# A ring of five row buffers in a graph kernel: two of them loaded from ScalarE's DMA queue instead of SyncE's

## The chip, the cores and the metric

The kernel runs on one core of one Trainium2 chip. The metric is device time in microseconds (us) of one execution. A core has five engines with instruction streams of their own: TensorE (PE in the profile), VectorE (DVE), ScalarE (ACT), GpSimd (POOL) and SyncE (SP). SP and ACT can both start DMA transfers; each has a queue of its own, which the profile calls q1 (SP) and q10 (ACT). The profile marks such issues as SPq and ACTq. The core has 16 DMA engines.

## The reference, cut to what matters

Four graph layers run one after another over 3125 nodes of 128 features and 103,125 edges. Each is followed by a residual and a layer norm. The change lies in the first one, a graph convolution (GCN):

```
def _L0_gnn_ref(x, edge_row, edge_col, edge_val, weight, b):
    xw = x @ weight
    msgs = edge_val[:, None] * xw[edge_col]
    out = jax.ops.segment_sum(msgs, edge_row, num_segments=N_NODES)
    out = jax.nn.relu(out + b)
    return out
...
x = _layernorm(x + _L0_gnn_ref(x, src, dst, edge_weight, ...), axis=-1)
x = _layernorm(x + _L1_gnn_ref(x, edge_index, ...), axis=-1)     # attention over edges (GAT)
x = _layernorm(x + _L2_gnn_ref(x, ..., edge_index), axis=-1)     # transformer-like attention
x = _layernorm(x + _L3_gnn_ref(x, edge_index, ...), axis=-1)     # two mean aggregations (SAGE)
```

## The kernel before, in words

The kernel turns the edge list into dense matrices. A first stage sorts out edge tables; a second builds, with one-hot matmuls, a matrix in DRAM that holds for each pair of nodes the number of edges and the sum of their weights. The two values are interleaved by runs of 100 columns, so one source row of weights is 32 runs of 100 floats (400 bytes each). The node count is padded to 3200, which gives NT = 25 row tiles of 128 rows.

The GCN sweep is the function `gcn_sums` (line 888) of `gcn_gat_rows`. For each of the 25 row tiles it multiplies the features of the tile's 128 source nodes with the tile's weights (128 x 3200) and adds up in the eight banks of PSUM, all of which it fills. In the profile these are 16 matmul records a tile at line 896. Three engines feed it:

- SP (lines 850 to 853) loads the tile's weights from DRAM, 1600 KB a tile, into a ring of UN = 5 buffers. Four are parts of `src_rows`, the fifth is a part of `count_t`, which is why the profile shows the loads and matmuls under two names. The issue of `load_rows` is line 683.
- POOL (lines 865 to 869) copies the tile's features into the ring `left`, also of five.
- PE (lines 891 to 898) waits for both, and adds one to `gcn_used` when it is done with a tile. `gcn_used` begins at 5, so the load and the copy of tile t wait until tile t - 5 is used up.

The loop runs over five laps of five tiles; buffer u holds tile lap * 5 + u. After its 25 loads SP goes on to `load(0, 0)` and `load(0, 1)`, the first two tiles of edge counts for the next layer (`count_pair` in the profile), and then waits for work of that layer.

ACT starts 14 small loads of weights and vectors at the head of the stage (lines 1170 to 1180), spreads a small vector (line 1183), loads the table for the square root (line 1185), and then waits until all 25 tiles are used (line 1186). With that it copies half of the sums out of PSUM (`take_sums`, line 1146), DVE the other half. From there on the next matmuls (line 902), the norm and the GAT layer follow.

In this text tile t means row tile t of the sweep, and 5k the first tile of lap k. The whole code of the functions around the change:

Of the kernel before, what the change touches and what calls it, by code (L numbers as in the profile page):

```python
# [25 lines left out]
NT = -(-N // P)  # L26
# [7 lines left out]
UN = 5  # L34
# [628 lines left out]
def hold(eng, sem, value, held):  # L663

    eng.wait_ge(sem, value)
    eng.sem_inc(held, 1)
# [14 lines left out]
def load_rows(sp, tile, matrix, t):  # L681

    return sp.dma_start(tile.rearrange("p (t h l) -> p t h l", t=1, l=SL), matrix[:, bass.ds(t, 1)])
# [14 lines left out]
def gcn_gat_rows(nc, k, heads, cols, e, count):  # L698

    with ExitStack() as ctx:  # L700
# [3 lines left out]
        def sem(name):  # L704
            return ctx.enter_context(nc.semaphore(name))
# [31 lines left out]
        ring = [src_rows[:, u, :] for u in range(HEADS)] + [  # L737
            count_t[:].rearrange("p t c -> p (t c)")[:, 0:NP]]
# [14 lines left out]
        gcn_in = [sem(f"gr_gcn_in{u}") for u in range(UN)]  # L753
# [23 lines left out]
        def is_super(g, which):  # L777
            return isinstance(g, int) and g == which

        def width(g):  # L780

            return 1 if is_super(g, LAST) else TWO
# [18 lines left out]
        def each_super(eng, work):  # L801

            work(0)
            with eng.Fori(1, LAST - 1) as g:
                work(g)
            work(LAST - 1)
            work(LAST)
# [7 lines left out]
        def counts_done(g):  # L815

            return g * 5 + (2 * width(g) + 1)

        @block.sync
        def _(sp):  # L820
            def load(g, j):
                load_rows(sp, count[:, j, :], k.count_rs, g * TWO + j).then_inc(loaded[j], 16)

            def store_node(g, h):
                n = TWO * (C + 1)
                hold(sp, kept, g * HEADS + (h + 1), held_sp)
                sp.dma_start(k.node_d[:, h, bass.ds(g * (TWO * (C + 1)), n)], node[:, h % TWO, 0:n]
                             ).then_inc(node_stored[h % TWO], 16)

            def super_tile(g):  # L830
                if not is_super(g, 0):
                    store_node(g - 1, HEADS - 1)
                if is_super(g, LAST):
                    for i in range(TWO):
                        sp.wait_ge(node_stored[i], LAST * TWO * 16)
                    sp.dma_start(count[:, 1, 0:HEADS * FULL_NODES].rearrange("p (h c) -> p h c", h=HEADS), k.node_d
                                 ).then_inc(nodes_in, 16)
                hold(sp, turned_n, counts_done(g), held_sp)
                hold(sp, masked, g * TWO + width(g), held_sp)
                if not is_super(g, LAST):  # L840
                    for j in range(width(g + 1)):
                        load(g + 1, j)
                hold(sp, taken_n, counts_done(g), held_sp)
                w = width(g) * P
                sp.dma_start(counts_out[:, :, bass.ds(g * WIDE, w)], count_t[:, :, 0:w]).then_inc(stored, 16)
                if not is_super(g, LAST):
                    for h in range(HEADS - 1):
                        store_node(g, h)

            with sp.Fori(0, NT // UN) as lap:  # L850
                for u in range(UN):
                    sp.wait_ge(gcn_used, lap * UN + (u + 1))
                    load_rows(sp, ring[u], k.weight_rs, lap * UN + u).then_inc(gcn_in[u], 16)
            load(0, 0)
            load(0, 1)
            each_super(sp, super_tile)
            sp.wait_ge(stored, SUPERS * 16)
            sp.wait_ge(nodes_in, 16)
# [217 lines left out]
        def _(act):  # L1076
# [67 lines left out]
            def take_sums(piece):  # L1144
                cut = slice(2 * piece * CW, 2 * (piece + 1) * CW)
                act.activation(agg[:, cut].rearrange("p (b c) -> p b c", c=CW), ps[:, 2 * piece:2 * piece + 2, 0:CW],
                               ACT.Copy).then_inc(sums_by_act, 1)
# [31 lines left out]
            for n, v in enumerate((k.L2_gnn_Wq, k.L2_gnn_Wk, k.L2_gnn_Wv, k.L2_gnn_Wo)):  # L1179
# [3 lines left out]
            act.activation(wide_watt[:], watt[:, 0:HEADS].unsqueeze(2).to_broadcast([P, HEADS, P]), ACT.Copy, scale=0.8  # L1183
                           ).then_inc(spread, 1)
            act.activation(out_t[:, 0:1], eps[:], ACT.Sqrt)
            act.wait_ge(gcn_used, UN + NT)
            take_sums(0)
            take_sums(2)
# [1168 lines left out]
```

## Time and profile before

| | us |
|---|---|
| median of 3 runs | 2210.5 |
| lowest, highest | 2206.9, 2212.16 |
| the profiled execution | 2211.6 |
| its span | 2209.8 |

| engine | busy us | share of the span |
|---|---|---|
| PE | 1856.7 | 84% |
| DVE | 1736.5 | 79% |
| ACT | 1195.8 | 54% |
| POOL | 120.4 | 5% |

The profile is that of one execution. The span goes from its first to its last instruction. The shares are averages over stages of different kinds; no engine is the busiest in all of them. Of the DMA traffic, 337.05 MB went through SP's queue and 2.20 MB through ACT's. The mean granted clock of PE was 0.958 of full speed. Rows of a timeline have the start and the length in us, then engine, line and operation, the tiles written and read, and in brackets the idle time before with what ended it.

### The profile page before, as it was taken

How to read it: one execution, taken by the hardware profiler on the slowest of the kernel's cores; microseconds unless marked ns; L12 is line 12 of the kernel's file. 1: busy time of each engine (PE TensorE's matmuls, PEld its weight loads, DVE VectorE, ACT ScalarE, POOL GpSimd, SP SyncE). 2: the span in 40 equal slices, each digit the busy share in tenths (PEclk: the TensorE clock that was granted, in tenths of full speed). 3: DMA queues.
4: the chain of work that ended last, by engine and by line, in shares of the span. 5: the costliest groups of instructions: out<-in, count | busy, mean ns of one | idle time of the engine just before them, and what ended most of it. 6: DMA issues, size and time to landing. Idle time of an engine off the chain costs nothing. (4 is left out here: it accounts for less than half of the span.)

```text
span 2209.8 us, 45503 instructions
## 1 busy us (share of the span) xinstructions
PE 1856.7 (84%) x17150; PEld 1419.5 (64%) x17151; DVE 1736.5 (79%) x1784; ACT 1195.8 (54%) x2210; POOL 120.4 (5%) x225
## 2 busy tenths in 40 slices
PE   3677776799788888988888888995899999799997
PEld 2666665444566666766676666774688888655655
DVE  5999997000689999999999999977688888677276
ACT  1666665000476777767776677765666666500202
POOL 4000000000000000000000000000000000011010
PEclk9999999899999999999999999985999999899999
DMA  4799998999043144413443144324355555299194
GB/s 114 220 255 255 256 256 231 264 272 272 4 121 81 43 120 120 120 31 91 120 120 69 54 121 120 92 62 102 78 119 119 119 119 149 100 380 392 56 404 165
DMA packets 482577, 341.91 MB, mean 155 GB/s; under 512 B 322696, under 2 KB 474528, under 8 KB 475856
## 3 DMA queue, kind: packets, MB, share of 16 engines
q1 hardware_dynamic: 476864, 337.05, 55.0%
q10 hardware_dynamic: 4928, 2.20, 0.4%
q0 software_dynamic: 720, 1.77, 0.3%
q8 instruction: 43, 0.70, 0.1%
q14 instruction: 22, 0.18, 0.0%
HBM read 214.05 MB, written 126.94 MB: 154 GB/s over the span
## 5 line engine op out<-in xcount | busy, mean ns | idle before, releaser
L1087 ACT ACTIVATE exponentials<-gr_ps,att_cols 128x256 f32<-128x256 f32 (+1 forms) x1300 | 486.7, 492 | 177.5 <-PE gr_ps L942 175.6
L942 PE MATMUL gr_ps<-ident,gr_r 128*128 128x128 f32 (+1 forms) x2500 | 369.2, 286 | 42.4 <-DVE gr_r L1293 40.3
L975 PE MATMUL gr_ps<-exponentials,heads 128*33 128x128 f32 (+1 forms) x5000 | 368.9, 283 | 35.2 <-DVE exponentials L1299 35.2
L1299 DVE SCALAR_TENSOR_TENSOR exponentials<-exponentials,gr_count_t 128x3072 f32<-128x3072 f32 (+1 forms) x104 | 344.0, 3307 | 25.8 <-ACT exponentials L1087 24.7
L1261 DVE CUSTOM_DVE_ANT_0 gr_unread<-gr_src_rows,gr_closed 128x3125 bf16<-128x3125 f32 (+1 forms) x100 | 341.3, 3413 | 17.2 <-ACT gr_src_rows L1141 12.5
L942 PEld LDWEIGHTS gr_ps<-ident,gr_r 128*128 128x128 f32 (+1 forms) x2500 | 274.3, 145 | 124.2 <-issue 105.7
L975 PEld LDWEIGHTS gr_ps<-exponentials,heads 128*33 128x33 f32 x5000 | 258.8, 115 | 103.3 <-issue 50.5
L577 PE MATMUL bm_ps<-bm_hot 128*96 128x100 bf16 x4224 | 223.6, 210 | 99.0 <-DVE bm_hot L527 99.0
L577 PEld LDWEIGHTS bm_ps<-bm_hot 128*96 128x96 bf16 x4224 | 206.4, 124 | 116.5 <-DVE bm_hot L527 116.5
L611 ACT ACTIVATE bm_stage<-bm_ps 96x800 f32<-96x800 f32 x264 | 207.1, 830 | 115.9 <-PE bm_ps L577 108.7
L527 DVE TENSOR_TENSOR bm_hot<-bm_hot,near 128x2304 bf16<-128x2304 bf16 x132 | 179.2, 1358 | 18.9
L1293 DVE TENSOR_SCALAR gr_r<-gr_src_rows,gr_bounds_u 128x3125 f32<-128x3125 f32 (+1 forms) x100 | 187.9, 1920 | 7.4 <-DVE gr_bounds_u L1280 4.0
L2035 PE MATMUL sage_ps<-sage_counts,sage_parts 128*128 128x400 bf16 x960 | 164.0, 332 | 0.0
L1574 PEld LDWEIGHTS ar_ps<-ar_values,ar_pt 128*128 128x128 f32 x1250 | 147.1, 194 | 11.2 <-ACT ar_pt L1655 2.5
L1574 PE MATMUL ar_ps<-ar_values,ar_pt 128*128 128x128 f32 x1250 | 149.4, 277 | 0.0
L1555 PE MATMUL ar_ps<-XT,ar_left 128*128 128x400 f32 x400 | 142.8, 500 | 1.9 <-issue 1.7
L2035 PEld LDWEIGHTS sage_ps<-sage_counts,sage_parts 128*128 128x128 bf16 x960 | 93.9, 98 | 68.5
L523 DVE TENSOR_TENSOR bm_hot<-low_grid,near 128x1600 bf16<-128x1600 int16 x132 | 130.0, 985 | 1.6 <-PEq L562 0.9
L896 PE MATMUL gr_ps<-gr_src_rows,exponentials 128*128 128x400 f32 x320 | 114.9, 514 | 17.0 <-DMA gr_src_rows<-adjacency 16.6
L1220 DVE COPY gr_r<-gr_ps 128x800 f32<-128x800 f32 x2 | 1.9, 986 | 155.3 <-PE gr_ps L896 155.3
L1655 ACT ACTIVATE ar_pt<-ar_ps 128x512 f32<-128x512 f32 (+1 forms) x175 | 82.5, 548 | 76.1 <-PE ar_ps L1564 76.1
L896 PEld LDWEIGHTS gr_ps<-gr_src_rows,exponentials 128*128 128x128 f32 x320 | 60.6, 194 | 71.4 <-issue 30.1
(307 smaller groups left out, 1998.7 us busy)
## 6 DMA issues: line engine op xcount, KB each, us to landing
adjacency<-bm_stage SPq DMA_DIRECT2D x264, 300.0 KB, 3.4
count_pair<-adjacency SPq DMA_DIRECT2D x37, 1600.0 KB, 8.5
count_more<-count_by_source SPq DMA_DIRECT2D x30, 1600.0 KB, 8.5
count_by_source<-gr_count_t SPq DMA_DIRECT2D x12, 3200.0 KB, 17.3
gr_src_rows<-adjacency SPq DMA_DIRECT2D x20, 1600.0 KB, 15.0
count_pair<-count_by_source SPq DMA_DIRECT2D x20, 1600.0 KB, 8.5
count_more<-adjacency SPq DMA_DIRECT2D x13, 1600.0 KB, 8.4
gr_count_t<-adjacency SPq DMA_DIRECT2D x5, 1600.0 KB, 15.0
```

The lines of the kernel that those rows point to most:

```text
L527: dve.tensor_tensor(planes(2, PARTS)[:, :, 0:KEYS], key.to_broadcast([P, PARTS, LW // 2, 2 * KEYS]), near(2, PARTS)[:, :, 0:KEYS], ALU.mul ...
L577: last = pe.matmul(place(i, plane), key, hot[:, u, 1, a, :, b], start=i % PER_BANK == 0 and plane == 0, stop=True, skip_group_check=True)
L611: act.activation(stage[:, u, HALF_LW * h:HALF_LW * (h + 1)].rearrange("p (b w) v c -> p b (w v c)", b=HALF_BANKS), ps[0:KEYS, bank:bank + ...
L896: last = pe.matmul(ps[:, b, 0:CW], left[:, u, :], ring[u][:, b * CW:(b + 1) * CW], start=False, stop=True, skip_group_check=True)
L942: last = pe.transpose(ps[:, i % RINGS, c:c + n], r[0:n, slot(g, h) + j, s * P:(s + 1) * P], k.ident[0:n, 0:n])
L975: last = pe.matmul(ps[j * PAIR:j * PAIR + C + 1, 7, 0:rows(g)], heads[:, h, s, :], e[:, s, c:c + rows(g)], start=s == 0, stop=s == NT - 1, ...
L1087: last = act.activation(e[:, s, places(g, h)], ps[:, i % RINGS, c:c + w], ACT.Exp, bias=cols[:, h, s:s + 1])
L1261: dve.tensor_tensor_reduce(out=unread[:, 0:n], in0=src_rows[:, h, 0:n], in1=closed[:, j, 0:n], scale=1.0, scalar=FLOOR, op0=ALU.subtract, ...
L1293: last = dve.tensor_scalar(r[:, slot(g, h) + j, 0:n], src_rows[:, h, 0:n], bounds_u[:, 1, h, j:j + 1], bounds_u[:, 0, h, j:j + 1], ALU.add ...
L1299: dve.scalar_tensor_tensor(part, part, 1.0, count_t[:, first:last, places(g, 0)], ALU.min, ALU.mult).then_inc(weighed, 1)
L1574: last = pe.matmul(ps[:, 7, 0:D], pt[:, i, j * P:(j + 1) * P], values[:, first + j, :], start=first + j == 0, stop=first + j == NT - 1, sk ...
L2035: last = pe.matmul(ps[:, b, 0:CW], part, right[:, columns(b)], start=opens and i == 0, stop=True, skip_group_check=True)
```

## The change

SP's loop over the ring now takes only the buffers 0, 2 and 4. ACT gets a loop of its own for the buffers 1 and 3, with the same waits, the same transfers and the same semaphores. It stands behind ACT's last preparation and ahead of its wait for the end of the sweep.

```diff
@@ -848,7 +848,7 @@
             with sp.Fori(0, NT // UN) as lap:
-                for u in range(UN):
+                for u in range(0, UN, 2):
                     sp.wait_ge(gcn_used, lap * UN + (u + 1))
                     load_rows(sp, ring[u], k.weight_rs, lap * UN + u).then_inc(gcn_in[u], 16)
             load(0, 0)
@@ -1183,6 +1183,10 @@
             act.activation(out_t[:, 0:1], eps[:], ACT.Sqrt)
+            with act.Fori(0, NT // UN) as lap:
+                for u in range(1, UN, 2):
+                    act.wait_ge(gcn_used, lap * UN + (u + 1))
+                    load_rows(act, ring[u], k.weight_rs, lap * UN + u).then_inc(gcn_in[u], 16)
             act.wait_ge(gcn_used, UN + NT)
             take_sums(0)
             take_sums(2)
```

What stands on SP at the end of its loop over the ring (`gr_src_rows` are buffers 0 to 3, `gr_count_t` is buffer 4):

```order
 L852 REGISTER_ALU
 L683 ISA [waits gr_gcn_used]
-L683 DMA gr_src_rows<-adjacency 128x32x100
-L852 REGISTER_ALU
-L683 ISA [waits gr_gcn_used]
-L683 DMA gr_src_rows<-adjacency 128x32x100
-L852 REGISTER_ALU
-L683 ISA [waits gr_gcn_used]
 L683 DMA gr_count_t<-adjacency 128x32x100
 L850 REGISTER_ALU
```

Two of the five loads of a lap have left SP, each with its wait. The count tiles that follow the loop stay where they were.

What stands on ACT between the square root's table load and its first copy of the sums:

```order
 L1185 ACTIVATE gr_out_t<-gr_eps 128x1
+L1186 UNCONDITIONAL_BRANCH
+L1186 ISA
+L683 ISA [waits gr_gcn_used]
+L683 DMA gr_src_rows<-adjacency 128x32x100
+L1188 REGISTER_ALU
+L683 ISA [waits gr_gcn_used]
+L683 DMA gr_src_rows<-adjacency 128x32x100
+L1186 REGISTER_ALU
+L1186 COMPARE_AND_BRANCH
 L1146 ACTIVATE gr_r<-gr_ps 128x800 [waits gr_gcn_used]
```

The loop body with two loads and two waits now stands where ACT had only the wait for the end of the sweep.

## Rows read from the trace of the kernel before

**Rows 1.** The page: span, and GB/s in 40 equal slices.
```profile
span 2209.8 us, 45503 instructions
...
GB/s 114 220 255 255 256 256 231 264 272 272 4 121 81 43 120 120 120 31 91 120 120 69 54 121 120 92 62 102 78 119 119 119 119 149 100 380 392 56 404 165
```

**Rows 2.** Windows in the sweep: stretch, length, busy time of engines, clock, DMA, GB/s.
```profile
core 0: us, PE busy (x) PEld busy (x) DVE busy (x) ACT busy (x) POOL busy (x), PEclk, DMA share, GB/s
...
420.00:450.00 30.00, 28.14 (x82) 14.75 (x81) 0.00 (x0) 0.00 (x0) 1.48 (x5) 1.00 1.28 273
...
510.00:540.00 30.00, 28.08 (x81) 14.73 (x80) 0.00 (x0) 0.00 (x0) 0.59 (x2) 1.00 1.29 272
```

**Rows 3.** Timeline of POOL in the sweep: start us, length us, what.
```profile
405.84 0.30 POOL L869 COPY exponentials<-X 128x128 f32 x1 [18.23 <-PE gr_ps L896]
411.31 0.30 POOL L869 COPY exponentials<-X 128x128 f32 x1 [5.18 <-PE gr_ps L896]
416.59 0.30 POOL L869 COPY exponentials<-X 128x128 f32 x1 [4.98 <-PE gr_ps L896]
...
512.46 0.30 POOL L869 COPY exponentials<-X 128x128 f32 x1 [5.72 <-PE gr_ps L896]
518.48 0.30 POOL L869 COPY exponentials<-X 128x128 f32 x1 [5.73 <-PE gr_ps L896]
```

**Rows 4.** Line 896, the sweep's matmuls: counts, and what they waited for.
```profile
L896 PE MATMUL gr_ps<-gr_src_rows,exponentials x320: 499/499/1031, 397.4 to 541.9; 128*128 128x400 f32 x160
...
  DMA gr_src_rows<-adjacency: 16.6, 16
```

**Rows 5.** SP's issues in the sweep, then the row loads to landing.
```profile
383.83 22.74 SPq L683 DMA_DIRECT2D gr_src_rows<-adjacency  x4
...
527.72 5.60 SPq L683 DMA_DIRECT2D gr_count_t<-adjacency  x1
...
L683 SPq DMA_DIRECT2D gr_src_rows<-adjacency x20: 667/5692/10325, 383.8 to 521.6; - x20
...
DMA to landing us min/median/max: 13.4/15.0/19.5
```

**Rows 6.** Timeline of PE: the sweep's first tiles, and its last.
```profile
397.36 24.71 PE L896 MATMUL gr_ps<-gr_src_rows,exponentials 128*128 128x400 f32 x64 [10.98 <-DMA gr_src_rows<-adjacency]
...
542.75 5.64 PE L896 MATMUL gr_ps<-gr_count_t,exponentials 128*128 128x400 f32 x16 [0.37 <-DMA gr_count_t<-adjacency]
```

**Rows 7.** Timeline of ACT around the sweep.
```profile
383.52 0.39 ACTq L1170 DMA_DIRECT2D gr_gcn_w<-in_L_gnn_weight_dram  x1
...
393.32 0.91 ACTq L1180 DMA_DIRECT2D wjoin<-in_L_gnn_Wo_dram  x1
...
396.27 0.20 ACT L1185 ACTIVATE gr_out_t<-gr_eps 128x1 f32<-128x1 f32 x1
548.42 1.57 ACT L1146 ACTIVATE gr_r<-gr_ps 128x800 f32<-128x800 f32 x2 [151.94 <-PE gr_ps L896]
```

**Rows 8.** Both queues at work: windows, then packets and MB of each in 4:5.
```profile
4.00:5.00 1.00, 0.00 (x0) 0.00 (x0) 0.00 (x0) 0.00 (x0) 1.00 (x5) 1.00 1.10 327
...
390.00:396.00 6.00, 0.00 (x0) 0.00 (x0) 1.29 (x7) 1.65 (x2) 0.00 (x0) 0.50 0.80 184
396.00:398.00 2.00, 0.64 (x1) 0.50 (x2) 0.00 (x0) 0.46 (x2) 0.00 (x0) 0.50 1.19 311
...
q1 hardware_dynamic: 334, 0.17, 56.3%
q10 hardware_dynamic: 307, 0.16, 53.2%
```

**Rows 9.** Timeline: the count tiles are used.
```profile
554.53 0.46 POOL L875 TENSOR_TENSOR count_pair<-count_pair,ident 128x128 f32<-128x128 f32 x1 [5.33 <-DMA count_pair<-adjacency]
...
559.85 2.95 ACT L1080 ACTIVATE gr_closed<-count_pair,gr_big 128x3200 bf16<-128x3200 f32 x1
```

## Prediction

> **What bounds the kernel now.** Start with the page: one core, a profiled execution of 2211.6 us with a span of 2209.8, so 1.8 us lie around the span, and the shown runs have their median at 2210.5, 1.1 below. In the page's line of GB/s [rows 1] the ninth and tenth of 40 slices sit at a flat 272, while later ones show anything from 4 to 404. Those are the GCN sweep, the only stretch that the change touches, so everything is read from there.
>
> The windows of that stretch [rows 2] give 272 to 273 GB/s over 30 us at the start and at the end of it, while PE is busy 28.1 of 30. PE is nearly full, but not full. The copies of POOL [rows 3] tell which of the two sets the pace, since each waits for the end of PE's 16 matmuls on one row tile (320 matmuls for the 20 tiles in the four slots of one tensor [rows 4]). Ends of tiles 0 to 2 lie 5.47 and 5.28 us apart, from 405.84 over 411.31 to 416.59, in a stretch where PE had tiles in hand: PE needs 5.38 us for a tile at full clock. Later the ends are 6.02 us apart (512.46 to 518.48). A tile is 1600 KB, 1.638 MB, and 1.638 MB at 272 GB/s is 6.02 us. So the sweep runs at the pace of the transfers, with 0.64 us of PE's time free in each tile. PE's idle time in front of these 20 tiles is only 16.6 us [rows 4], 11.0 of it the wait for the first load [rows 6].
>
> SP's own rows [rows 5] show its loads issued without a pause: the median issue takes 5.69 us, one right behind another, and a load lands 15.0 us after its issue (median). So an issue on SP is held until an earlier load has been moved, and SP runs behind the ring, not PE: POOL's copy shows slot 4 free for tile 24 at 518.48, SP issues that tile at 527.7 [rows 3, 5]. After its last tile SP issues the two count tiles for the next stage. PE ends the sweep at 548.39 (542.75 + 5.64), and ACT, which has waited 151.9 us for that, goes on at 548.42 [rows 6, 7]. Nothing else runs past this point: the next layer's matmuls wait for those copies, so what PE's end of the sweep moves, the whole rest moves with it.
>
> **The change part by part.** It takes 10 of 25 load issues from SP and gives them to ACT, with the same waits. No byte, matmul or buffer changes.
>
> *ACT's time.* 10 issues of up to about 6 us each lie in the 151.9 us in which ACT did nothing. The last is tile 23, over long before PE ends. Cost nothing; the loop's register instructions too. If that cover went, ACT's copies behind it would be late, and PE and all after it with them; nothing in the arithmetic below comes near.
>
> *SP's time.* SP's issues were held by transfers, and with fewer of them it still has the next tile's issue ready. This gives nothing by itself: the transfers were already without gaps [rows 2].
>
> *The first loads.* Before, tile 1 was issued behind tile 0 at about 384.5. Now it stands behind 14 small loads, the wait for the watt steps and the table load on ACT, so it is issued after 396.5 [rows 7] and shares the bandwidth with tile 2. At half of 272 GB/s a load takes 12.04 us, so tile 1 lands near 410, while PE ends tile 0 at about 405 [rows 3]: a new wait of some 5 us. By itself it is made up, since the transfers go on and PE is the faster of the two.
>
> *The rate with both queues at work.* The trace of before has no two big row loads in two queues. The nearest rows are these. At the kernel's start both queues load edge lists, 334 packets and 307 in one microsecond, an even split at a sum of 327 GB/s with packets of 512 B [rows 8]: 641 packets per us, where the sweep's 400 B packets make 680 (272 GB/s by 400 B). At the sweep's start, with small loads on ACT's queue, the sum is 184 GB/s over 390 to 396 and 311 over 396 to 398 [rows 8]. So the unknown lies between 184 and 311 at its ends. I take 272, the plain sweep's value: the packets per us of both steady cases are alike, 641 and 680, and the low value goes with separate small commands, the high one with 2 us after a slack stretch. And I take an even split between the queues, as at the start.
>
> The Trainium skill, "DMA: Bandwidth & Descriptors", section "Issuing engines are not separate DMA queues", speaks against the change: transfers started by several engines run on the same 16 DMA engines and interleave, and only the sequencer's issue time is saved. By that rule the sweep's rate stays as it is; the split of 334 to 307 agrees, no steady stretch here shows the rate itself.
>
> *The order of arrival.* This is where equal bandwidth costs time. SP's queue now carries tiles 5k, 5k+2, 5k+4 and ACT's 5k+1, 5k+3. So 5k+4 and the next lap's first tile follow each other on SP at half rate, while ACT at its half rate brings tiles that PE needs later. I walked the 25 loads with these rules: 272 GB/s split evenly while both queues have work, whole to one otherwise, 1.5 us from the last byte to the landing, a tile issued when its slot is free, 5.38 us per tile on PE, 8.0 for the first at the low clock (the 1.5 and the 8.0 are my estimates; the trace has 8.5 from the first matmul to 405.84). For the kernel of before the walk has tile 20 landed at 516.7 and PE's end at 546.2 (the trace: 548.4, so only differences are used). With two queues, tile 20's transfer starts at 512.9, after 19, and takes 12.04: it lands at 526.4. By then ACT has moved all of tile 21 and 0.65 of 23, 1.65 loads out of turn, which at 6.02 each are the 9.7 to 9.9 us. From there PE finds each tile there and needs 5 x 5.38, ending at 553.4. The free 0.64 in each of four tiles has given back 2.6 of the 9.7. **Sum: +7.1 us.** With the split between 45 and 55 per cent, or the first wait left out, the walk gives +5 to +9.
>
> *The count tiles.* They come behind SP's last tile as before, and the walk has them land at the same times to 0.2 us. POOL adds to the second at 554.53, ACT's mask comes at 559.85, 5 us later, and moves back by 7 itself [rows 9]. Nothing.
>
> *The clock.* It was at half (1.2 GHz) when the sweep began, after PE had waited 11 us (0.50 in the window 396:398 of [rows 8]), and at full (2.4 GHz) in both windows of [rows 2]. PE's idle time now comes in lumps of up to 6 us instead of 0.4 to 0.7. A lump that drops the clock would cost up to 5 us for the tile behind it; in the walk this changes the end by -3 to +3, since the transfers go on. I leave it out and widen.
>
> **The rivals.**
>
> *A, the forecast*, equal rate and even split: +7.1, so 2218.7 against the profiled execution and 2217.6 against the median.
>
> *B, two queues move more than one.* For it: 327 and 311 GB/s in stretches with both queues at work [rows 8]. Against: they are 1 to 2 us long, and the steady sweep has no gaps to fill. Break-even is where the faster transfers pay for the order, near 288 GB/s in the walk. At 311 a load takes 5.27 us, less than PE's 5.38, so PE is the bound from tile 1's landing at about 410 on, apart from a few order waits: the walk ends 6 to 10 earlier, 2202 to 2204. The floor, with no wait at all after 410, is 410 + 24 x 5.38 = 539.1, 7 below the walk's 546.2, or 12 below were tile 1 there at 405.
>
> *C, whole loads in turn.* If a load once begun keeps the other queue out, the split is not by halves but by turns: tile 5k then waits for one load out of turn, 6.0 us, less the 2.6: +3.4, so 2214. Against: ACT issued its 14 small loads between 383.5 and 394.2 while one of SP's row loads was in issue for 10.3 us [rows 5, 7], which a lock by whole loads would not let pass, and in one microsecond at the kernel's start both queues moved a like number of packets [rows 8]. The Trainium skill, "Perfetto Trace Analysis", section "DMA Instruction — HWDGE (DVE, Sync)", says that the descriptor generator is locked for exclusive use by one instruction, which is this rival. The trace does not agree as it stands.
>
> *D, two queues at work move less.* It speaks for it that the 6 us in which both engines issued gave 184 GB/s, and that SP's issue took 10.3 instead of 5.7 us. Against it: those were many small commands. It decides from 272 down: at 240 GB/s a load takes 6.83 us and the walk ends 25 later (2236); at 190 it takes 8.62, 2.6 more for each of some 23 loads, +60 (2270).
>
> *E, nothing happens*: the order settles so that PE never misses a tile, as when ACT's queue, held by full slots, gives way. Then 2210 to 2212.
>
> **How the numbers follow.** A change under 0.2%, 4.4 us, can't be told from none here. Chances: A 0.42, B 0.22, C 0.13, D 0.16, E 0.07. Faster by over 0.2% is B without its weakest part, 0.20. Within it are C, E, the edge of A and a little of B: 0.28. Slower is most of A, and D: 0.52. The time is A's, 2217.6, its own range 2214 to 2221. The range over all cases: down to 2200, which takes in nearly all of B, and up to 2238, which takes in D to a combined rate of about 240 GB/s and leaves out its rest, about one in ten.
>
> **What would show it.** In the profile of the changed kernel: the windows from 420 to 540 still at 272 GB/s (above 288: B; below 265: D). PE's waits in the sweep gathered at one tile per lap, several us each, before tiles 10, 15 or 20, not 0.4 in each (A); half as large in C. Tile 1 starting near 410. Landing times of single loads grown from 15.0 to 16 to 28 us. ACT's first copy after the sweep near 555 instead of 548.4, and every later stage as before, moved by that. The forecast is wrong if the rate changes with two queues, or if the queues don't share by halves.

## The result

| | before | after |
|---|---|---|
| median of 20 runs each, us | 2206.87 | 2213.22 |
| lowest, highest | 2203.45, 2213.03 | 2209.03, 2219.88 |
| span of the profiled execution | 2209.8 | 2207.3 |
| ACT's first copy after the sweep | 548.42 | 552.18 |

The ratio is 1.0027, with an interval of 1.0018 to 1.0036: slower by 6 us, 4 to 8. The forecast was +7.1. The two spans say the opposite of the medians, so the first thing to read is where a single execution can be trusted. The sweep ends 3.8 us later in the profile of after. Behind it, before's span had 1661.4 us left (2209.8 less 548.42) and after's 1655.1. Over the profiles of this study that rest lies between 1653 and 1663 whatever is done to the sweep; before's is among the longest. So the sweep's end is compared by profile, the whole by medians.

The sweep's end has a scatter of its own, and it comes from the stage's start. The run e1_again below is the changed kernel once more. These are the bytes that moved from 383 to 420 us in before, in the changed kernel, and in its second profile:

```profile
DMA packets 22178, 8.92 MB, mean 241 GB/s; under 512 B 20511, under 2 KB 22175, under 8 KB 22175
DMA packets 22880, 9.21 MB, mean 249 GB/s; under 512 B 21213, under 2 KB 22877, under 8 KB 22877
DMA packets 22246, 8.95 MB, mean 242 GB/s; under 512 B 20579, under 2 KB 22243, under 8 KB 22243
```

The 0.26 MB between the two profiles of one kernel are 1.0 us at 272 GB/s, and their sweeps end 1.1 us apart (552.18 and 553.28). So the first of them had a lead of 1.1 us over this profile of before (0.29 MB), which hides a part of what the change cost: 4.8 us instead of 3.8 when the lead is added. This sum is an estimate, and so are those of the second table with the experiments.

The windows of the changed kernel, to be read against [rows 2]:

```profile
core 0: us, PE busy (x) PEld busy (x) DVE busy (x) ACT busy (x) POOL busy (x), PEclk, DMA share, GB/s
408.00:414.00 6.00, 3.06 (x5) 1.75 (x6) 0.00 (x0) 0.00 (x0) 0.00 (x0) 0.59 1.29 272
420.00:450.00 30.00, 30.00 (x91) 16.99 (x90) 0.00 (x0) 0.00 (x0) 1.47 (x5) 1.00 1.29 272
450.00:480.00 30.00, 27.38 (x81) 15.03 (x80) 0.00 (x0) 0.00 (x0) 1.47 (x5) 1.00 1.30 272
480.00:510.00 30.00, 27.26 (x77) 15.15 (x76) 0.00 (x0) 0.00 (x0) 1.47 (x5) 0.94 1.29 272
510.00:540.00 30.00, 28.63 (x85) 15.71 (x84) 0.00 (x0) 0.00 (x0) 0.88 (x3) 1.00 1.29 272
```

The last column is 272 in every window. Two queues move what one moved. How they share it, from the DMA view of 420 to 450 (q1 is SP's queue, q10 ACT's; packets, MB, share of the engines' time):

```profile
DMA packets 20490, 8.16 MB, mean 272 GB/s; under 512 B 20490, under 2 KB 20490, under 8 KB 20490
q1 hardware_dynamic: 11452, 4.56, 72.3%
q10 hardware_dynamic: 9038, 3.60, 57.2%
```

SP got 56% and ACT 44% over these 30 us. That mixes stretches in which both queues have work with others in which one is empty, because its next slot isn't free. Short windows tell them apart. From 453 to 456, and then from 504 to 507:

```profile
q1 hardware_dynamic: 1022, 0.41, 65.5%
q10 hardware_dynamic: 1020, 0.41, 64.1%
...
q1 hardware_dynamic: 2045, 0.82, 129.9%
```

With work in both queues each moves half of the packets, and it does so within 3 us, half the time of one load at the full rate. From 504 to 507 ACT's queue moves nothing, and SP's has the whole rate. Tile 21, ACT's next, could only be issued at 507.44, when tile 16 was used, and its first packets moved near 509.

PE in the sweep, against [rows 6]; each row is a run of matmuls, 16 to a tile, the bracket is the idle time before it:

```profile
397.06 8.22 PE L896 MATMUL gr_ps<-gr_src_rows,exponentials 128*128 128x400 f32 x16 [10.90 <-DMA gr_src_rows<-adjacency]
410.94 18.86 PE L896 MATMUL gr_ps<-gr_src_rows,exponentials 128*128 128x400 f32 x48 [5.65 <-DMA gr_src_rows<-adjacency]
...
435.00 21.66 PE L896 MATMUL gr_ps<-gr_src_rows,exponentials 128*128 128x400 f32 x64
...
464.65 21.91 PE L896 MATMUL gr_ps<-gr_src_rows,exponentials 128*128 128x400 f32 x64 [2.62 <-DMA gr_src_rows<-adjacency]
...
494.67 23.33 PE L896 MATMUL gr_ps<-gr_src_rows,exponentials 128*128 128x400 f32 x64 [2.74 <-DMA gr_src_rows<-adjacency]
...
524.27 11.01 PE L896 MATMUL gr_ps<-gr_src_rows,exponentials 128*128 128x400 f32 x32 [0.89 <-DMA gr_src_rows<-adjacency]
535.76 11.01 PE L896 MATMUL gr_ps<-gr_src_rows,exponentials 128*128 128x400 f32 x32 [0.48 <-DMA gr_src_rows<-adjacency]
546.61 5.54 PE L896 MATMUL gr_ps<-gr_count_t,exponentials 128*128 128x400 f32 x16
```

Before had a wait of 0.4 us ahead of almost each tile. Now PE runs five to nine tiles without one and then waits at the tiles 1, 10, 15 and 20, which are the ones at 410.94, 464.65, 494.67 and 524.27. The waits are 5.65, 2.62, 2.74 and 0.89 us. In before the tile that starts the last lap stands at 518.70:

```profile
518.70 5.63 PE L896 MATMUL gr_ps<-gr_src_rows,exponentials 128*128 128x400 f32 x16 [0.39 <-DMA gr_src_rows<-adjacency]
```

So tile 20 is 5.6 us late, and the end 3.8, less than tile 20, since PE spent 5.4 us on most of the later tiles, where before's transfers allowed one each 6.02. It is not for want of bytes: from 383 to 520 us the changed kernel moved 36.40 MB and before 36.13. ACT's copy, and the view of the row loads in the sweep:

```profile
552.18 1.56 ACT L1146 ACTIVATE gr_r<-gr_ps 128x800 f32<-128x800 f32 x2 [156.74 <-PE gr_ps L896]
```

```profile
L683 SPq DMA_DIRECT2D gr_src_rows<-adjacency x10: 543/6674/8157, 383.6 to 512.8; - x10
L683 ACTq DMA_DIRECT2D gr_src_rows<-adjacency x10: 550/562/10377, 393.7 to 518.2; - x10
...
DMA to landing us min/median/max: 13.3/18.0/28.2
```

A load now takes up to 28.2 us to land, against 19.5 in [rows 5]. Most of ACT's issues return in 0.56 us: its queue has room, where SP's issues in before took 5.69 us (median) behind an earlier load.

### The profile page after: what moved, and what is told of

It is laid out like the page before. It is cut to its first block and busy times, and to the rows that moved or that the text cites. A ratio compares the mean times of both kernels' runs of the same rounds, so it can differ in the third digit from the quotient of the medians.

```text
span 2207.3 us, 45516 instructions
## 1 busy us (share of the span) xinstructions
PE 1849.1 (84%) x17150; PEld 1417.2 (64%) x17151; DVE 1736.6 (79%) x1784; ACT 1194.0 (54%) x2210; POOL 118.1 (5%) x225
## 5 line engine op out<-in xcount | busy, mean ns | idle before, releaser
L896 PE MATMUL gr_ps<-gr_src_rows,exponentials 128*128 128x400 f32 x320 | 116.0, 524 | 23.3 <-DMA gr_src_rows<-adjacency 23.3
```

Of the source, the lines that this page charges most:

```text
L896: last = pe.matmul(ps[:, b, 0:CW], left[:, u, :], ring[u][:, b * CW:(b + 1) * CW], start=False, stop=True, skip_group_check=True)
```

## The experiments

All are compared with before on the same chip. "Sweep's end" is ACT's first copy of the sums in the profile; before has 548.42.

| run | ratio to before (interval) | sweep's end |
|---|---|---|
| e1_again | 1.0016 (1.0003 to 1.0029) | 553.28 |
| e2_lap0_sp | 1.0024 (1.0010 to 1.0037) | 551.66 |
| e3_two_laps | 0.9986 (0.9975 to 0.9998) | 548.18 |
| e4_swap1 | 1.0000 (0.9987 to 1.0014) | 551.76 |
| e12_swap1_again | 1.0022 (1.0007 to 1.0036) | 550.94 |
| e7_swap2 | 1.0110 (1.0093 to 1.0126) | 571.61 |
| e10_last_lap | 1.0053 (1.0033 to 1.0073) | 558.61 |
| e5_small_behind | 0.9991 (0.9982 to 1.0001) | 546.67 |
| e6_halves | 1.0011 (0.9998 to 1.0024) | 552.39 |
| e9_halves_hold | 1.0012 (0.9999 to 1.0025) | 550.24 |
| e8_next_on_sp | 0.9984 (0.9975 to 0.9992) | 544.45 |
| e11_all_on_sp | 0.9973 (0.9962 to 0.9985) | 543.17 |

For the runs that keep the small loads where before has them, the lead at 420 us can be taken into account as above:

| profile | MB moved 383 to 420 | lead on before, us | sweep's end, later than before | with the lead added |
|---|---|---|---|---|
| before | 8.92 | | | |
| after | 9.21 | 1.1 | 3.8 | 4.8 |
| e1_again | 8.95 | 0.1 | 4.9 | 5.0 |
| e2_lap0_sp | 9.29 | 1.4 | 3.2 | 4.6 |
| e3_two_laps | 9.17 | 0.9 | -0.2 | 0.7 |
| e4_swap1 | 9.03 | 0.4 | 3.3 | 3.7 |
| e12_swap1_again | 9.15 | 0.8 | 2.5 | 3.4 |
| e7_swap2 | 8.94 | 0.1 | 23.2 | 23.3 |
| e10_last_lap | 9.34 | 1.5 | 10.2 | 11.7 |

The two profiles of the changed kernel agree within 0.2 us that way, and those of e4 and e12 within 0.3, where they were 1.1 and 0.8 apart.

**e1_again**, the changed kernel unedited.

> The changed kernel once more, for a second profile beside the experiments. In the profile of it that exists, the sweep (ACT's first copy at 552.18, before 548.42) ends 3.8 us later and the rest of the span is 6 us shorter, while the medians differ by 6.3. Order theory: the sweep again ends 3 to 7 us later than before's 548.4, at 272 GB/s, with PE's waits gathered before tiles 1, 10, 15, 20; time +4 to +7. If the rest of the program is also changed by the edit (rival), the span behind the sweep differs from before in the same direction again.

PE and ACT in this profile:

```profile
412.23 17.88 PE L896 MATMUL gr_ps<-gr_src_rows,exponentials 128*128 128x400 f32 x48 [7.02 <-DMA gr_src_rows<-adjacency]
...
526.12 21.76 PE L896 MATMUL gr_ps<-gr_src_rows,exponentials 128*128 128x400 f32 x64 [3.22 <-DMA gr_src_rows<-adjacency]
...
553.28 1.57 ACT L1146 ACTIVATE gr_r<-gr_ps 128x800 f32<-128x800 f32 x2 [156.74 <-PE gr_ps L896]
```

Tile 20 at 526.12, 7.4 late, the end 4.9 late: the same pattern with other numbers. The time is 3.5 us up, 0.7 to 6.4, which overlaps the first measurement. The rest behind the sweep was short again, 1653.1, but so it is in e4 (2204.9 less 551.76), which has nothing on ACT's queue. The edit does not do that.

**e2_lap0_sp**: does the late tile 1 cost the time?

```
+ for t in [t for t in range(NT) if t < UN or t % UN in (0, 2, 4)]:      # SP
+ for t in [t for t in range(UN, NT) if t % UN in (1, 3)]:               # ACT
```

> Tiles 0 to 4 all on SP as before, ACT takes tiles 5k+1 and 5k+3 only from tile 6 on. Order theory (loads out of turn in laps 1 to 4 make tile 5k late, what counts is the lateness of tile 20): the walk gives tile 20 at +9 and the end at +6, as for the changed kernel, so +4 to +7 us. Rival, late start (the cost is the 5.65 us wait for tile 1 and the 8.3 us that tile 1 takes at the half clock): the wait is gone, so 0 to +1 us.

The wait for tile 1 is gone, but a wait of 7.4 us for tile 4 came in its place, again with a slow tile behind it (7.2 us). The last lap is nearly as late as in the changed kernel:

```profile
396.80 23.99 PE L895 MATMUL gr_ps<-gr_src_rows,exponentials 128*128 128x400 f32 x64 [10.59 <-DMA gr_src_rows<-adjacency]
428.21 7.24 PE L895 MATMUL gr_ps<-gr_count_t,exponentials 128*128 128x400 f32 x16 [7.42 <-DMA gr_count_t<-adjacency]
...
523.75 11.01 PE L895 MATMUL gr_ps<-gr_src_rows,exponentials 128*128 128x400 f32 x32 [0.80 <-DMA gr_src_rows<-adjacency]
...
551.66 1.57 ACT L1145 ACTIVATE gr_r<-gr_ps 128x800 f32<-128x800 f32 x2 [156.66 <-PE gr_ps L895]
```

+5.3 us by the ratio (2.2 to 8.2), where the late-start rival gave 0 to 1. Tile 1's wait as such is not the cost. A late start of another kind was still there, so it takes the next run to put the rival out.

**e3_two_laps**: two queues in laps 0 and 1, SP alone from tile 10.

```
+ for t in [t for t in range(NT) if t >= 2 * UN or t % UN in (0, 2, 4)]: # SP
+ for t in [t for t in range(2 * UN) if t % UN in (1, 3)]:               # ACT
```

> The two queues share laps 0 and 1 only, tiles 10 to 24 are all on SP. The late tile 1 and its half clock stay. Order theory: tile 10 is late, then PE makes up 0.64 us a tile, so by tile 24 nothing is left: the walk ends where before ends, 0 to +1 us. Late-start rival: +4 us or more, as in the changed kernel. A rival by which the second queue costs something for each load: 4 loads of 10, so about +1.6 to +2.5.

```profile
411.37 17.92 PE L895 MATMUL gr_ps<-gr_src_rows,exponentials 128*128 128x400 f32 x48 [6.36 <-DMA gr_src_rows<-adjacency]
...
494.44 5.64 PE L895 MATMUL gr_ps<-gr_src_rows,exponentials 128*128 128x400 f32 x16 [0.37 <-DMA gr_src_rows<-adjacency]
...
542.51 5.64 PE L895 MATMUL gr_ps<-gr_count_t,exponentials 128*128 128x400 f32 x16 [0.39 <-DMA gr_count_t<-adjacency]
```

The early wait is there, from tile 16 on (the row at 494.44) PE is back at the pace of the transfers, and the last tile starts within 0.3 us of before's 542.75 [rows 6]. Lateness early in the sweep is given back; only what is late at the end counts. That puts the late start out as a cause. The time came out 3 us below before, 0.4 to 5.5, where 0 to +1 was expected. The sweep's end shows only 0.2 of that, or +0.7 with the lead at the start added, and the rest is not explained.

**e4_swap1 and e12_swap1_again**: the wrong order in one queue.

```
+ for t in [0, 1, 2, 3, 4, 6, 5, 7, 8, 9, 11, 10, 12, 13, 14, 16, 15, ...]:  # SP alone
```

> One queue only, but SP issues tile 5k+1 ahead of tile 5k in laps 1 to 4. Order theory: tile 20 arrives one load (6.02 us) late, four tiles give back 0.64 each, so the walk gives +3.5 us with the rate at 272 GB/s and no second queue. Rivals (late start, or a cost of the second queue itself): 0 to +1 us.

> One queue, tile 5k+1 ahead of 5k, once more. Its profile had the sweep's end 3.3 us later, as the walk has it (+3.5), but its time was that of before (ratio 1.0000, 0.9987 to 1.0014). If the sweep's end is passed on, this time gives +1 to +5 us; if it is lost behind the sweep, 0 again, with the span behind the sweep shorter than in the other profiles by 3 us.

From e4's profile:

```profile
524.60 21.76 PE L895 MATMUL gr_ps<-gr_src_rows,exponentials 128*128 128x400 f32 x64 [1.28 <-DMA gr_src_rows<-adjacency]
```

Without a second queue tile 20 starts 5.9 us late, one load's time, and the sweep ends 3.3 and 2.5 us late, with +3.5 expected. The times are 0 (-2.9 to +3.1), a miss, and +4.9 (+1.5 to +7.9). The first left open whether the sweep's end is passed on, the second says that it is. Together they are near +2.4, and the two intervals overlap.

**e7_swap2**: two loads out of turn in one queue.

```
+ for t in [0, 1, 2, 3, 4, 6, 7, 5, 8, 9, 11, 12, 10, 13, 14, 16, 17, 15, ...]:  # SP alone
```

> One queue only, SP issues tiles 5k+1 and 5k+2 ahead of 5k in laps 1 to 4. Order theory: tile 20 arrives two loads late; the walk gives +10.3 us, three times the +3.5 of the run with one load out of turn (12.04 less 2.6 would be 9.4). Rival: lateness is hidden by the ring of five, 0 to +2.

+24 us (20.5 to 27.8), and the sweep's end 23.2 late, where +10.3 was expected. The direction held, the size did not. The stretch from 420 to 540, PE at tile 20 and at tile 5, and SP's issues of tile 9 and of the next lap:

```profile
420.00:540.00 120.00, 95.76 (x264) 52.53 (x262) 0.00 (x0) 0.00 (x0) 5.04 (x17) 0.89 1.15 245
```

```profile
542.18 24.01 PE L895 MATMUL gr_ps<-gr_src_rows,exponentials 128*128 128x400 f32 x64 [4.65 <-DMA gr_src_rows<-adjacency]
```

```profile
440.56 23.63 PE L895 MATMUL gr_ps<-gr_src_rows,exponentials 128*128 128x400 f32 x64 [12.38 <-DMA gr_src_rows<-adjacency]
```

```profile
437.21 5.91 SPq L683 DMA_DIRECT2D gr_count_t<-adjacency  x1
453.47 17.30 SPq L683 DMA_DIRECT2D gr_src_rows<-adjacency  x4
```

The rate fell to 245 GB/s, so here the transfers did have gaps. PE could start tile 5 only at 440.56. By then the ring was full, and SP's next load in its order, tile 11, needed the slot of tile 6: SP issued nothing from 443.1 to 453.47, though tile 5's slot was free before. The clock was at 0.89 over the stretch, and four tiles took 24.0 us where the changed kernel needed 21.7 for the same 64 matmuls (at 435.00). How the 13 us above the forecast divide between the gaps and the clock was not tested.

**e10_last_lap**: ACT loads only tiles 21 and 23.

```
+ for t in [t for t in range(NT) if t < 4 * UN or t % UN in (0, 2, 4)]:  # SP
+ for t in [t for t in range(4 * UN, NT) if t % UN in (1, 3)]:           # ACT
```

> ACT loads only tiles 21 and 23, all else is SP's. Order theory: SP still has tiles 18 to 20 ahead in its queue when ACT starts 21, so tile 20 is late by about two loads and nothing is left to make it up in: the walk gives +9.5 us, more than with ten loads on ACT. Rival, a cost for each load on the second queue or for the start: 2 of 10 loads, 0 to +1.3 us.

```profile
517.16 7.06 PE L895 MATMUL gr_ps<-gr_count_t,exponentials 128*128 128x400 f32 x16 [5.16 <-DMA gr_count_t<-adjacency]
529.24 23.97 PE L895 MATMUL gr_ps<-gr_src_rows,exponentials 128*128 128x400 f32 x64 [5.01 <-DMA gr_src_rows<-adjacency]
553.04 5.54 PE L895 MATMUL gr_ps<-gr_count_t,exponentials 128*128 128x400 f32 x16
```

```profile
498.62 13.96 ACTq L683 DMA_DIRECT2D gr_src_rows<-adjacency  x2
```

Two loads on ACT cost more than ten: +11.7 us (7.3 to 16.1), the sweep's end 10.2 late, or 11.7 with the start's lead added; +9.5 was expected. ACT's queue was empty, so tile 21, issued at 498.62, had half the rate from about 503 on, while SP still had 18, 19 and 20 to bring. Tile 23 followed at 512.0; the row covers both issues and the wait between them. A price for each load on a second queue is ruled out by this run and e3 together.

**e5, e6 and e9**: both queues, right order. e5 is one queue, with ACT's small loads behind tile 0 (`act.wait_ge(gcn_used, UN + 1)` ahead of them). e6 loads columns 0 to 15 of the 32 runs of each tile on SP and 16 to 31 on ACT:

```
+ sp:  load_half(sp, ring[t % UN], k.weight_rs, t, 0).then_inc(gcn_in[t % UN], 16)
+ act: load_half(act, ring[t % UN], k.weight_rs, t, 1).then_inc(gcn_in[t % UN], 16)
+ pe.wait_ge(gcn_in[u], lap * 32 + 32)
```

e9 adds `sp.wait_ge(gcn_used, UN + 22)` ahead of SP's count tiles.

> One queue for the tiles as before, but ACT's 14 small loads wait until PE has used tile 0, so that tile 0 is loaded alone. Serves as the base for the next run. Tile 0 should land at about 392 instead of 397; the small loads' bytes still take their share later. The walk ends 3.1 us earlier than before, so -2 to -4 us. If the slow stretch of 184 GB/s at the start is caused by the small loads beside a row load wherever they are, it only moves: 0 to -1.

> Each tile is loaded as two halves of its columns, one on SP, one on ACT, from tile 0 on, the small loads behind ACT's first five halves. Both queues are at work through the whole sweep, but tiles arrive in order. Order theory: rate 272 GB/s, no lumps of PE waiting, the end as in the run with the small loads behind tile 0, so -2 to -4 us against before. If two queues cost something by themselves, by transfers or by switching, it is slower than that base by 4 us or more.

> The kernel with each tile in two halves, but SP's two count tiles wait until PE has used tile 21. Why: in the run before, SP ran ahead of ACT, whose queue had lost time to the 14 small loads; PE still got a tile every 6.02 us, but 5.7 us late, and SP's count tiles (issued at 525.1, from 525 on beside ACT's last halves) moved about one load's worth of bytes ahead of tile 24. If that reading is right, all bytes go to the tiles that PE waits for, and ACT's first copy after the sweep comes at 546 to 548 us instead of 552.4, the time 3 to 6 us below the halves run (-2 to -4 against before). If the second queue costs time by itself, the copy stays at 551 to 553.

e5 ends its sweep at 546.67, and its time is -2.0 us (-4.0 to +0.2). e6 was expected there and ended at 552.39, as late as the changed kernel; its median is 5.7 us above e5's. The expectation had called 4 us or more a sign that two queues cost something by themselves, so by its own test that rival was not out. PE at tile 20 in e5, then from e6's profile PE at tile 20 and SP's count tiles:

```profile
516.91 5.64 PE L896 MATMUL gr_ps<-gr_src_rows,exponentials 128*128 128x400 f32 x16 [0.39 <-DMA gr_src_rows<-adjacency]
```

```profile
522.64 5.63 PE L901 MATMUL gr_ps<-gr_src_rows,exponentials 128*128 128x400 f32 x16 [0.40 <-DMA gr_src_rows<-adjacency]
```

```profile
525.11 17.88 SPq L683 DMA_DIRECT2D count_pair<-adjacency  x2
```

After a wait of 8.5 us for tile 5 PE gets a tile every 6.02 us there, without lumps, but all of them are late: tile 20 by 5.7 against e5's 516.91. My halves left the small loads in ACT's queue, so SP's halves ran ahead of ACT's, as far as the ring lets them, and a tile needs both. The bytes bear this out. From 383 to 520 us e6 moved 36.74 MB, more than e5 (36.62), so the second queue cost no rate. But SP's queue had moved 18.63 MB of halves, and ACT's 18.07, of which 0.85 were the small loads: SP was 1.4 MB ahead. With an even share ACT would have been 0.7 MB further, 0.86 of one of its halves, and as a tile comes each 6.02 us that is 5.2 of the 5.7 us (an estimate from these numbers). At the end SP's head start went into count tiles, issued 8 us sooner than in before, which PE doesn't need yet. e9 held those back. PE's last tiles there:

```profile
527.80 5.64 PE L902 MATMUL gr_ps<-gr_src_rows,exponentials 128*128 128x400 f32 x16 [0.39 <-DMA gr_src_rows<-adjacency]
533.83 11.01 PE L902 MATMUL gr_ps<-gr_src_rows,exponentials 128*128 128x400 f32 x32 [0.38 <-DMA gr_src_rows<-adjacency]
544.67 5.54 PE L902 MATMUL gr_ps<-gr_count_t,exponentials 128*128 128x400 f32 x16
```

Behind tile 22, at 533.83, PE no longer waits, and the sweep ends 2.1 us sooner than e6, at 550.24, where 546 to 548 was expected. Tile 22 was 4.9 late against e5's 528.95, and three tiles give back under 2, so 3.6 were left. The times of e6 and e9, +2.4 and +2.6, don't tell the two apart, and e9's was expected at -2 to -4. So the reading of e6 is supported by the bytes in its trace and by 2.1 of the 4.4 to 6.4 us expected of e9; a split in which both queues keep step wasn't tried, and it stays open whether that would cost nothing.

**e8 and e11**: what the sweep's start holds. e8 moves the 9 small loads that only later stages need from ACT's head to SP, behind the count tiles. e11 moves all 14 to SP, 5 between tile 24 and the count tiles:

```
  SP: 25 tiles
+     gcn_w, gcn_bias, mixing, att x2
      load(0, 0); load(0, 1)
+     skip_w, vecs x4, wjoin x4
  ACT: (none of these), the spread of the small vector behind the sums and the relu
```

> One queue for the tiles as before, but the 9 small loads that only the next stages need (skip weights, vectors, projections, 0.59 MB) are moved from ACT's head to SP behind the two count tiles. The sweep has 0.59 MB less to move, 2.2 us at 272 GB/s, and less of the slow stretch at its start: -2 to -5 us against before. If those bytes and the slow stretch are hidden anyway: 0.

> One queue, nothing else in it ahead of the tiles: all 14 small loads go to SP, 5 between tile 24 and the count tiles, 9 behind these; ACT spreads its small vector after the sums. The step from the 9 moved loads gave the sweep's end at 544.45. Another 0.26 MB, 1 us, leaves the sweep, and tile 0 lands at about 392. Sweep's end 543 to 544, -3 to -6 us against before, if ACT's later spread is hidden. If the weights come late for the layer at 545, 0 to +2.

```profile
390.00:396.00 6.00, 3.86 (x6) 2.18 (x7) 0.00 (x0) 0.00 (x0) 0.00 (x0) 0.50 1.30 272
```

e11 has 272 GB/s where [rows 8] had 184. That 184 is the low end: the eight other profiles that have the small loads in this place had 222 to 259 in the same window. The first tile of e11 starts 5 us sooner than in this profile of before, and the sweep ends at 543.17, 5.3 us before before's; against a start like e10's it is nearer 4 (an estimate: 5.3 less the lead of 1.5). Both are faster than before, by 3.5 us (1.8 to 5.5) and 6.0 us (3.3 to 8.4). e11 is faster than before, and the changed kernel is slower than before, so e11 beats both kernels.

## Why the prediction was right

Point by point, by its steps.

- *The rate.* Taken as 272 out of 184 to 311; it is 272 in each 30 us of the changed kernel. The rivals with more (B) or less (D) bandwidth are out, and E, no change, by both intervals of the time. The Trainium skill, "DMA: Bandwidth & Descriptors", section "Issuing engines are not separate DMA queues", states that transfers run on the same 16 DMA engines whichever engine started them. The trace agrees: the same 272 GB/s from one queue and from two.
- *The split.* Taken as even, and it is: 1022 packets to 1020 in 3 us while both queues have work. This is what puts rival C out, whole loads in turn, since such a turn would fill 6 us with one queue's packets. The time could not have done it: C gave +3.4, and the two measurements are 6.0 and 3.5. Nor could the waits of 2.6 and 2.7 us at the tiles 10 and 15, since C was to have waits half as large as A's "several us". The prediction's own argument against C was weaker than it says. Its SP issue of 10.3 us began at 390.47, so only the last three or four of ACT's 14 issues fall into it, and the others into the issue before.
- *The order of arrival.* Lumps of waiting at tiles 1, 10, 15 and 20 as forecast, though at tile 20 only 0.89 us in one profile (3.22 in the other), since PE itself had been late with the lap before. That lateness at the end is the cause, and not the second queue, is shown from three sides: the same in one queue with one load out of turn (e4, e12), none when only the early laps are mixed (e3), and more with only two loads moved, if they are the last (e10).
- *The size.* +7.1 was somewhat too much. The times moved by 6.0 and 3.5, the sweep's end by 3.8 and 4.9 in two profiles, or 4.8 and 5.0 with the lead at the start added. The mis-sized term is tile 20's lateness: 9.7 in the walk, 5.6 and 7.4 in the traces, or 6.7 and 7.5 with the lead. The give-back was forecast as 2.6 and measured 1.8 and 2.5. What the traces show is that ACT's queue was empty ahead of tile 20 (no packet from 504 to 507, and none from 506 to 510 in e1), which gave SP the whole rate for tiles that PE needed. The walk lacks two things that lengthen such a gap. One is the clock, which fell after PE's waits (0.59 over 408 to 414, 0.94 over 480 to 510): tile 1 took 8.3 us and tile 15 took 7.4, so the slots behind them came free later. The walk done over with these two lengths comes out about 2 us lower, nearly all of it from tile 15, whose lateness holds back the slots of tiles 20 and 21 (an estimate; no run tests it). In e1_again the slow tile was tile 10. The other is the time from an issue into an empty queue to its first packets: tile 21 was issued at 507.44, and from 507.4 to 508.8 all packets were still SP's, where the walk lets a load start at once. How much each of the two is worth is argued, not tested.
- *The time itself.* 2213.22 was measured against 2217.6 forecast, just under A's own range of 2214 to 2221. 3.6 us of that are before's median, which was 2210.5 over the 3 runs shown and 2206.87 over 20.
- *The first wait.* Forecast as 5 us and made up later: 5.65, and e3 keeps it (6.36 there) and loses nothing.
- *Count tiles and ACT's time.* Costless, as said. POOL's addition to the second count tile came at 553.47, ACT's mask only at 563.60.
- *The signs named in advance.* "Near 555" for ACT's first copy was 552.18 and 553.28. The landing times, 15.0 grown "to 16 to 28", have a median of 18.0 and reach 28.2.

## What to carry to other kernels

Here the transfers already ran without gaps, and a second queue added no bandwidth; it only changed in which order the bytes arrived, and bytes that overtook the ones that were waited for were paid. Where the reader of a ring is a little faster than its loads, as PE was here, early lateness is given back, and what is left at the end is paid: ask what has overtaken the last tiles. Look at what else is in the queues at the stage's start and end: here moving small loads out of the way gave 6 us, as much as the change cost. And before reading 4 us out of one profile, compare two profiles of the same program: here the sweeps of one kernel ended 1.1 us apart.

## What the runs showed of the hardware that was not expected

- Small loads beside a row load cost more than their bytes, and not the same each time: 184 to 259 GB/s over 390 to 396 in the nine profiles that have them there (184 in [rows 8]), 272 in the same window once they are gone (e11). With one queue or two, row loads alone gave 272 wherever loads were waiting; in e7, where SP had to hold its issues, it was 245.
- A wait of 5.65 us on PE was followed by the half clock (1.2 GHz): 0.59 over 408 to 414, and tile 1 took 8.3 us instead of 5.4. The waits of 0.4 us in before were followed by none.
- Two queues with row loads in both share by halves, 1022 packets to 1020 in 3 us, though their loads were issued at different times.
- A row load issued into an empty queue moved its first packets only after a while: issued at 507.44, none by 508.8; in e10 issued at 498.62, none by 502.
